# Time mixing beside small experts on one Trainium2 core: keys and decay computed once per chunk and spread through a DRAM scratch

## What is computed

```python
delta = shifted - x                      # shifted: the token before, zero at a sequence's start
low = jnp.tanh((x + delta * mu_x) @ W_x1).reshape(B, T, 5, PROJ_LR)
mus = jnp.einsum('blnr,dnr->blnd', low, W_x2) + x_bias
xr, xw, xk, xv, xg = [x + delta * mus[:, :, i] for i in range(5)]
r, k, v = xr @ W_r, xk @ W_k, xv @ W_v   # r, k: 16 heads x 4 keys; v: 16 heads x 8 values
w = -jnp.exp(jnp.tanh(xw @ W_w1) @ W_w2 + b_w2)
def step(S, inp):                        # S: 16 heads x 4 keys x 8 values
    r_t, k_t, v_t, w_t = inp
    o_t = jnp.einsum('bhk,bhkv->bhv', r_t, S) + jnp.einsum('bhk,hk,bhk,bhv->bhv', r_t, u, k_t, v_t)
    S = jnp.exp(w_t)[..., None] * S + k_t[..., :, None] * v_t[..., None, :]
    return (S, o_t)
# o: per head minus its mean, over its standard deviation; then
o = (o * gn_w + gn_b) * (g * jax.nn.sigmoid(g))      # g = xg @ W_g
return o @ W_o
```

## Time and profile before

| | us |
|---|---|
| runs shown | 4533.47, 4528.71, 4528.97 |
| median | 4528.97 |
| span of the profiled execution | 4561.0 |
| the last stage in it, from its first transfer issue (3721.9) | 839.1 |
| its 264 steps, first to last silu (3771.3 to 4545.2) | 773.9 |

### The profile page before, as it was taken

One profiled execution on the slowest core, in us unless ns is written; L12 is line 12 of the kernel. 1 busy time (PEld: TensorE's weight loads), 2 busy tenths in 40 slices (PEclk: granted clock), 3 DMA queues, 4 the chain that ended last, 5 costly groups with the idle time before them and its releaser, 6 DMA issues. The chain is left out here.

```text
span 4561.0 us, 88454 instructions
## 1 busy us (share of the span) xinstructions
PE 4030.3 (88%) x34698; PEld 2244.0 (49%) x34700; DVE 3477.9 (76%) x4781; ACT 2975.3 (65%) x4498; POOL 2360.6 (52%) x1443
## 2 busy tenths in 40 slices
PE   6999999999998989996877778887888868999998
PEld 3666666766676644451121211345777443444443
DVE  6888888888884557767889897466777747888888
ACT  3777777777775459953777777674565716555555
POOL 2878888888884013330221110461667526666665
PEclk7999999999999989986899999898999979999999
DMA  2212221221220011100210100331000323343433
GB/s 82 58 41 56 58 51 43 58 57 46 50 48 1 1 63 55 69 19 12 77 67 27 40 26 7 120 106 50 13 14 14 102 91 96 93 103 94 102 94 88
DMA packets 112123, 261.46 MB, mean 57 GB/s; under 512 B 24020, under 2 KB 35668, under 8 KB 110236
## 3 DMA queue, kind: packets, MB, share of 16 engines
q1 hardware_dynamic: 96292, 215.01, 17.3%
q0 software_dynamic: 15424, 40.89, 2.7%
HBM read 170.31 MB, written 49.76 MB: 48 GB/s over the span
## 5 line engine op out<-in xcount | busy, mean ns | idle before, releaser
L522 POOL TENSOR_TENSOR a_prob_low<-a_prob_whole,a_prob_high 128x1024 f16<-128x1024 f32 x512 | 1084.4, 2130 | 277.1 <-ACT a_prob_high L412 277.1
L496 DVE TENSOR_REDUCE a_part_max<-a_top 128x2 f32<-128x1024 f32 x512 | 626.2, 1223 | 218.3 <-PE a_top L323 212.4
L409 ACT ACTIVATE a_prob_whole<-a_score 128x1024 f32<-128x1024 f32 x512 | 524.9, 1025 | 332.5 <-PE a_score L312 320.4
L976 ACT ACTIVATE a_prob<-a_score 128x512 f32<-128x512 f32 x1024 | 533.1, 604 | 256.6 <-PE a_score L915 256.5
L1009 DVE TENSOR_REDUCE a_part_max<-a_side 128x2 f32<-128x1024 f32 x512 | 595.1, 1219 | 68.5 <-PE a_side L886 68.0
L2172 POOL TENSOR_TENSOR m_scaled<-m_acted,m_gate 128x512 f32<-128x512 f32 x264 | 433.2, 1649 | 269.4 <-DVE m_acted L2290 200.7
L412 ACT ACTIVATE a_prob_high<-a_score 128x1024 f16<-128x1024 f32 x512 | 522.3, 1020 | 0.0
L311 PE MATMUL a_score<-a_qa,a_ka 128*128 128x256 f16 x2048 | 476.1, 273 | 0.0
L312 PE MATMUL a_score<-a_qb,a_kb 128*128 128x256 f16 x2048 | 475.8, 273 | 0.0
L378 PE MATMUL a_o_ps<-a_v,a_prob_high 128*128 128x65 f16 x4096 | 428.7, 193 | 6.0 <-POOL a_prob_low L522 3.3
L380 PE MATMUL a_o_ps<-a_v,a_prob_high 128*128 128x64 f16 x4096 | 427.6, 194 | 0.0
(11 more groups left out here) (483 smaller groups left out, 10371.7 us busy)
## 6 DMA issues: line engine op xcount, KB each, us to landing
m_gate<-gates SPq DMA_DIRECT2D x264, 256.0 KB, 5.0
a_ka<-a_nat_high_k SPq DMA_DIRECT2D x128, 128.0 KB, 2.4
e_gate<-gates SPq DMA_DIRECT2D x8, 2048.0 KB, 7.1
slots<-in_slots SPq DMA_DIRECT2D x19, 520.0 KB, 4.3
a_qa<-a_nat_high_q SPq DMA_DIRECT2D x64, 128.0 KB, 2.4
a_qa<-a_nat_low_q SPq DMA_DIRECT2D x64, 128.0 KB, 2.4
a_qb<-a_nat_high_q SPq DMA_DIRECT2D x64, 128.0 KB, 2.4
a_kb<-a_nat_low_k SPq DMA_DIRECT2D x64, 128.0 KB, 2.4
```

The source lines that it names most:

```text
L409: eng.activation(prob_whole[:, e % RING, :, :, :], score[:, e % 2, :, :, :], ACT.Exp, scale=scale)
L496: eng.tensor_reduce(part_max[:, i, c, :, qt % 4], top[:, :, :], AX.X, ALU.max).then_inc(max_done, 1)
L522: eng.tensor_tensor(prob_low[:, e % RING, :, :, :], prob_whole[:, e % RING, :, :, :], prob_high[:, e % RING, :, :, :], ALU.subtract).then_ ...
L976: eng.activation(prob[:, e % RING, h, :], score[:, step % SLOTS, :], ACT.Exp).then_inc(exp_done, 1)
```

## The change

- r, k, w and v are made once per chunk: four matmuls (`w`, `k`, `r`, `v`) where there were 16; r, k and w fill 64 partitions (16 heads x 4 keys), v 128.
- ACT writes decay, k and r into `keys` [64 x 3 x 512] (`ew`, `decay`, `kc`, `rc`). SP stores it to a DRAM tensor `keys_d` (384 KB) and loads it back as `rep` [128 x 4 groups x 3 x 512] (3072 KB), each row of a head broadcast to its 8 value partitions. The loads of gate rows are now issued from a walk over the slots in which these two transfers have their places.
- `kv`j multiplies k in `rep` by `vs` in place, and `scan`j and `rs`j read decay and r from `rep`. `rs`j is the state times r alone.
- The term with u leaves the groups: `ruk` = r u k on 64 partitions (DVE), `bonus` sums it per head (PE), `av` = that times v (DVE), `oa` adds it into `o_ps`.
- `pick` becomes `center` (identity minus the mean over a head's 8 values), so `o_ps` is centred as it is accumulated: `o`, `mean` and `cen` go. `sq` reads `o_ps`; `eps` becomes the bias of `std`; the reciprocal is made in two halves; `norm` reads `o_ps`; `affine` moves to ACT. The group norm closes at slots 30 to 40 of the chunk, `LAST` goes, `PERIOD` is 33.

```diff
-    START, PERIOD = 12, 34
+    START, PERIOD = 12, 33
     PE_AT = {"low": 0, "low5": 1, "mu1": 2, "mu3": 3, "mu2": 4, "tanh_w": 5, "mu0": 6, "mu4": 7,
-             "w0": 8, "w1": 9, "v0": 10, "w2": 11, "w3": 12, "k0": 13, "r0": 14, "v1": 15, "k1": 16, "r1": 17, "o0": 18,
-             "v2": 19, "k2": 20, "r2": 21, "o1": 22, "v3": 23, "k3": 24, "r3": 25, "o2": 26, "g": 27, "o3": 28,
-             "mean": 30, "var": 33, "out": 63}
+             "w": 8, "k": 9, "r": 10, "v": 11, "g": 12, "bonus": 13, "o0": 23, "o1": 25, "o2": 27, "o3": 29, "oa": 30,
+             "var": 32, "out": 39}
-    ACT_AT = {"low": 1, "low5": 2, "wt": 6, "ew0": 10, "ew1": 10, "decay0": 10, "decay1": 10, "vs0": 11,
-              "ew2": 13, "ew3": 13, "decay2": 13, "decay3": 13, "vs1": 16, "vs2": 20, "vs3": 24,
-              "gs": 28, "o": 29, "sq": 32, "std": 36}
+    ACT_AT = {"low": 1, "low5": 2, "wt": 6, "ew": 9, "decay": 9, "kc": 10, "rc": 11, "vs": 12, "gs": 13,
+              "sq": 31, "std": 33, "affine": 37}
-    DVE_AT = {"z": -1, "mixed1": 3, "mixed3": 4, "mixed2": 5, "mixed0": 7, "mixed4": 8,
-              "kv0": 14, "carry0": 14, "scan0": 14, "u0": 15, "rs0": 15, "kv1": 17, "carry1": 17, "scan1": 17, "u1": 18, "rs1": 18,
-              "kv2": 21, "carry2": 21, "scan2": 21, "u2": 22, "rs2": 22, "kv3": 25, "carry3": 25, "scan3": 25, "u3": 26, "rs3": 26,
-              "cen": 31, "eps": 34, "rstd": 43, "norm": 45, "affine": 45, "gated": 47, "res": 64}
+    DVE_AT = {"z": -1, "mixed1": 3, "mixed3": 4, "mixed2": 5, "mixed0": 7, "mixed4": 8, "ruk": 12, "av": 14,
+              "carry": 19, "kv0": 20, "scan0": 21, "kv1": 22, "rs0": 22, "scan1": 23, "kv2": 24, "rs1": 24,
+              "scan2": 25, "kv3": 26, "rs2": 26, "scan3": 27, "rs3": 28,
+              "rstd0": 34, "rstd1": 35, "norm": 36, "gated": 38, "res": 40}
-    LAST = {"std": 35, "rstd": 36, "norm": 36, "affine": 36, "gated": 36, "out": 38, "res": 39}
+    KEEP_AT, SPREAD_AT = 12, 13
...
+                    c = (slot - KEEP_AT) // PERIOD
+                    if (slot - KEEP_AT) % PERIOD == 0 and c < CH:
+                        if c:
+                            eng.wait_ge(rep_in, 16 * c)
+                        after_act(eng, "rc", c)
+                        eng.dma_start(keys_d[:, :], keys[:, :, :]).then_inc(keys_out, 16)
+                    c = (slot - SPREAD_AT) // PERIOD
+                    if (slot - SPREAD_AT) % PERIOD == 0 and c < CH:
+                        after_dve(eng, "rs3", c - 1)
+                        eng.wait_ge(keys_out, 16 * (c + 1))
+                        eng.dma_start(rep[:, :, :], keys_d.rearrange("(h k) t -> h k t", k=GROUPS).unsqueeze(1).broadcast_to([16, 8, GROUPS, 3 * BANK])).then_inc(rep_in, 16)
...
-                        eng.matmul(o_ps[:, :], const["pick"][:, j, :], rs[:, j % 2, :], start=j == 0, stop=j == GROUPS - 1).then_inc(pe_done, 1)
+                        after_dve(eng, "av" if name == "oa" else f"rs{j}", c)
+                        eng.matmul(o_ps[:, :], const["center"][:, :], av[:, :] if name == "oa" else rs[:, j % 2, :],
+                                   start=name == "o0", stop=name == "oa").then_inc(pe_done, 1)
...
+                    elif name == "ruk":
+                        after_act(eng, "rc", c)
+                        after_pe(eng, "low5", c)
+                        op = eng.scalar_tensor_tensor(out=z[0:KEYS, :], in0=keys[:, W_R, :], scalar=cols[0:KEYS, U:U + 1],
+                                                      in1=keys[:, W_K, :], op0=ALU.mult, op1=ALU.mult)
...
-                        op = eng.tensor_tensor(kv[:, :], work[:, bank_of[f"k{j}", c], :], vs[:, j % 2, :], ALU.mult)
+                        if j == 0:
+                            after_act(eng, "vs", c)
+                            eng.wait_ge(rep_in, 16 * (c + 1))
+                        op = eng.tensor_tensor(rep[:, j, W_K * BANK:(W_K + 1) * BANK], rep[:, j, W_K * BANK:(W_K + 1) * BANK], vs[:, :], ALU.mult)
...
-                        op = eng.tensor_tensor_scan(st[:, j, 1:BANK + 1], decay[:, j, :], kv[:, :], st[:, j, 0:1], ALU.mult, ALU.add)
+                        op = eng.tensor_tensor_scan(st[:, j, 1:BANK + 1], rep[:, j, W_DECAY * BANK:(W_DECAY + 1) * BANK], rep[:, j, W_K * BANK:(W_K + 1) * BANK], st[:, j, 0:1], ALU.mult, ALU.add)
-                    elif name[0] == "u":
...
-                        op = eng.tensor_tensor(rs[:, j % 2, :], rs[:, j % 2, :], work[:, bank_of[f"r{j}", c], :], ALU.mult)
+                        op = eng.tensor_tensor(rs[:, j % 2, :], st[:, j, 0:BANK], rep[:, j, W_R * BANK:(W_R + 1) * BANK], ALU.mult)
...
+                        half = slice(j * BANK // 2, (j + 1) * BANK // 2)
+                        op = eng.reciprocal(std[:, half], std[:, half])
```

More of the change, by code:

```diff
@@ L1816, in mixing_and_experts @@
         gs = pl.sb("gs", [P, BANK])
-        vs = pl.sb("vs", [P, 2, BANK])
-        decay = pl.sb("decay", [P, GROUPS, BANK])
-        kv = pl.sb("kv", [P, BANK])
+        vs = pl.sb("vs", [P, BANK])
+        keys = pl.sb("keys", [KEYS, 3, BANK])
+        rep = pl.sb("rep", [P, GROUPS, 3 * BANK])
+        av = pl.sb("av", [P, BANK])
         st = pl.sb("st", [P, GROUPS, BANK + 1])
         rs = pl.sb("rs", [P, 2, BANK])
-        oz = pl.sb("oz", [P, BANK])
         cen = pl.sb("cen", [P, BANK])
-        sq = pl.sb("sq", [P, BANK])
         std = pl.sb("std", [P, BANK])
@@ L1880, in after_pool, with wait_bank @@
                 eng.wait_ge(pool_done, pool_no[name, c])
-        READER = {"low": (after_act, "low"), "low5": (after_act, "low5"), "tanh_w": (after_act, "wt"), "g": (after_act, "gs"),
-                  "mean": (after_dve, "cen"), "var": (after_dve, "eps"), "out": (after_dve, "res")}
-        READER.update({f"mu{i}": (after_dve, f"mixed{i}") for i in range(5)})
-        READER.update({f"{p}{j}": by for j in range(GROUPS) for p, by in
-                       (("w", (after_act, f"ew{j}")), ("v", (after_act, f"vs{j}")), ("k", (after_dve, f"kv{j}")), ("r", (after_dve, f"rs{j}")))})
+        def wait_bank(eng, name, c):
+            if (name, c) not in bank_user:
+                return
+            user, at = bank_user[name, c]
+            if user in IN_ACT:
+                after_act(eng, IN_ACT[user], at)
+            if user in IN_DVE:
+                after_dve(eng, IN_DVE[user], at)
+        IN_ACT = {"low": "low", "low5": "low5", "tanh_w": "wt", "w": "ew", "k": "kc", "r": "rc", "v": "vs", "g": "gs", "var": "std"}
+        IN_DVE = {"mu0": "mixed0", "mu1": "mixed1", "mu2": "mixed2", "mu3": "mixed3", "mu4": "mixed4", "bonus": "av", "out": "res"}
         def step_at(slot, lag):
@@ L1902, in store, with gate_rows @@
                     eng.dma_start(gates_d[:, pair * PAIR:(pair + 1) * PAIR], gates_t[:, pair % 2, :]).then_inc(stored[pair], 16)
-                for pair in range(2):
-                    store(pair)
-                for n in range(UNITS):
-                    for pair in range(CH // 2):
-                        g = n * (CH // 2) + pair
+                def gate_rows(g):
+                    n, pair = g // (CH // 2), g % (CH // 2)
+                    for j in range(J):
+                        for e in range(2):
+                            row = gates_d[2 * J * n + 2 * j + e:2 * J * n + 2 * j + e + 1, pair * PAIR:(pair + 1) * PAIR]
+                            eng.dma_start(gate[e * 64:e * 64 + 64, g % 2, j, :], row.broadcast_to([64, PAIR])).then_inc(gate_in[g % 2], 16)
+                store(0)
+                store(1)
+                eng.wait_ge(stored[0], 16)
+                gate_rows(0)
+                eng.wait_ge(stored[1], 16)
+                store(2)
+                store(3)
+                gate_rows(1)
+                for slot in range(SLOTS):
+                    g = (slot - START - UP_LAG) // (2 * J) + 1
+                    if (slot - START - UP_LAG) % (2 * J) == 0 and 2 <= g < UNITS * CH // 2:
+                        n, pair = g // (CH // 2), g % (CH // 2)
                         if n == 0:
                             eng.wait_ge(stored[pair], 16)
-                        if g == 1:
-                            store(2)
-                            store(3)
                         if pair == 2 and n + 1 < UNITS:
@@ L1916, in _ @@
                             eng.dma_start(w[:, :, :], w_d[n + 1, :, :, :]).then_inc(w_in, 16)
[L1917 to L1922 removed]
+                        eng.wait_ge(scaled_done, 2 * J * (g - 1))
+                        gate_rows(g)
+                    c = (slot - KEEP_AT) // PERIOD
[9 more added lines that the diff above has]
+                        eng.dma_start(rep[:, :, :], keys_d.rearrange("(h k) t -> h k t", k=GROUPS).unsqueeze(1).broadcast_to([16, 8, GROUPS, 3 * BANK])).then_inc(rep_in, 16)
                 for c in range(CH):
@@ L3023, in program @@
         sent2 = [pl.sem(f"sent2{r}") for r in range(2)]
+        keys_d = nc.dram_tensor("keys", (64, 3 * BANK), F32, kind="Internal").ap()
```

188 lines of the change are left out of this document (88 added, 100 removed).

## The result

The kernel after takes 4565.74 us (median of 4 runs, 4559.30 to 4573.47), the kernel before, beside it on the same chip, 4530.89 (4 runs, 4528.71 to 4533.47). The ratio is 1.0079, with a 95% interval of 1.0067 to 1.0091: slower by 0.8%, some 35 us, where 4510 was forecast. It lies above the range (4475 to 4548), on the side of rival (a).

A forecast was written before the change was run, and what follows sets the result against it. PE was taken to set the pace, with DVE a second bound right behind. Steps -13.5, end -7.3, start -1 and transfers +3 made -18.8: 4561.0 becomes 4542.2 profiled, 4510 from the median 4528.97; range 4475 to 4548.

The forecast's parts named there:

- rival (a): At kv0, `rep` arrives late from about 200 GB/s down; at 150 GB/s 70 us instead of 3, so 4577; chance 0.13.
- the steps: The last stage's 264 steps, first to last silu: 760.4 us against 773.9 before, a gain of 13.5.
- The end: After the last silu: 8.5 us with hand-overs instead of 15.8, a gain of 7.3.
- Slots 20 to 28: The stretch with kv, scans and rs: DVE sets the pace, 32.3 us per chunk, of which PE needs 20.0.
- the exclusion: A DVE operation with two SBUF operands and POOL's L2172 exclude each other; DVE pays about 1.20 us per slot waiting.
- Slots 29 to 13: Into the next chunk, 18 steps and 18 mixing matmuls: PE needs 50.4 us, DVE's 38.2 stays under it.
- the 3.5 of losses: Time lost per chunk beyond the engines' work: 3.5 us kept of 7.0, bounds 1.5 and 6.5.
- Slots 14 to 19: Six slots without mixing matmuls on PE: 6 x 1.94 = 11.6 us per chunk.
- The start: DVE's first z waits for the last constant; smaller constants gain 1 us, bounds 0 and 3.
- The transfers: Store of `keys`, load of `rep` at 405 GB/s: stalls of 0 to 2 us in chunks 2, 4, 6; +3 us.
- Rival (b), the clock: In slots 20 to 28 PE gets half the clock: +7.8 us per chunk, 4572; chance 0.07.
- Rival (c): No change: losses at their upper bound cost 24 us more; half of that gives 4520 to 4538; chance 0.22.

The follow-up runs named there:

- the kernel with both repairs: Changed kernel with `rep` loaded in four 768 KB loads, each with its own count, and the next unit's weights issued behind the earlier gate rows: 4521.70 us, ratio 0.9985.

## Why the prediction was wrong, step by step

Its own sum, made against the profile: the steps 760.4 with transfers left out, +3 for these, start -1, end -7.3.

- **The end** (-7.3): measured -7.2. Right.
- **Slots 20 to 28** (32.3): 31.5 in chunk 3 of after, where nothing is waited for, and 30.9 to 33.2, 31.9 on average, over the eight chunks of the kernel with both repairs. Right, and for the reason given: `kv` 1.75, scan 2.28, `rs` behind `kv` 0.68, DVE busy 31.50 of 31.50 in chunk 3. The run with v in PSUM agrees: without the reason the stretch is shorter by what its price says. Its -3 us per chunk was there to be found in the rows, and the prediction, which worked the exclusion out, didn't see that one operand left in PSUM avoids it.
- **Slots 29 to 13** (52.8 with the crossing and the 3.5 of losses): 51.8 to 53.3. Right.
- **Slots 14 to 19** (11.6): 12.5 to 13.5, 15.1 in chunk 3 even when its weights come in time. Too low: slot 14 takes 2.80 us from L2318 to L2318 and not 1.94, which is one mixing matmul (0.86) of slot 13 that lies on this side of the cut; the remaining 0 to 1 us per chunk, and 2.6 in chunk 3, isn't accounted for. The period without late transfers is then (4381.3 - 3891.3) / 5 = 98.0 us over chunks 2 to 6 of the kernel with both repairs, and not 96.7. Put to the term of the losses, which the sum had at 3.5 us a chunk, the 1.3 us make it 4.8, within its bounds of 1.5 and 6.5; that is 769.3 instead of 760.4 us of steps.
- **The start** (-1): +6.3. Missed outright. The prediction looked only at the wait for the constants; in the new order the first step stands behind chunk 0's k and r, which now come in slots 9 and 10, one bank after the other: DVE waited 9.1 us with `ruk` for `rc`, and `rc` 5.5 for PE (shown above). Every engine's first steps are in its queue behind this.
- **The transfers** (+3, bounds -3 to +25): 41.7 by the steps (811.0 - 769.3), 44.0 by the medians. This is the step that failed, in two places. The rate: the prediction chose the row of `e_gate`, 405 GB/s, because it too fills 128 partitions, over the 215 of the gate rows, and it wrote itself that the load "has a destination and a source like no other here". It priced the lower rate only at the stall of chunks 2, 4 and 6, from which came an upper bound of 25. At 206 GB/s `rep` takes 15.3 us and not 7.8. With a round of gate rows ahead of it in chunks 2, 4 and 6 DVE's waits there come to 25.4; for the other chunks the prediction had room, and they waited 11.1 in four. In chunk 1 `rep` is issued 5.5 us behind the store and not some 4 behind `rc`, and `kv0` starts 18 us after that. What PE and ACT lose before they are back in step comes on top of these 36.5. The queue: "in SP's queue the next gate rows stand behind `rep`", it says, and leaves out the load that also stands there in chunk 3, that of the weights: 26.0 us where the run that moves it has 15.1, and 12 to 13 us of the whole time by that run.
- **Rival (a)** named the place (`kv0`), the sign and the point from which it decides (about 200 GB/s). The measured 206 lies at that point, not at 150, and the time at 4566, not 4577. The chance of 0.13 was low for a cost whose nearest rows lay at 215 and 405, with the point of decision at 200 just below the lower one.
- **Rival (b), the clock:** the granted clock kept 1.00 through stretches with PE busy 21.9 of 31.5 and 23.0 of 32.8 us, and fell, to 0.92 and 0.77, only where PE sat through a wait; it was 0.97 in the stretch behind the longest. Right to give it little.
- **Rival (c)** is what the change is once its transfers are in time: 4521.7 to 4533 in the runs that repair or remove them, against 4529.

In the profiled executions the stage was to be 18.8 us shorter and was 36.2 longer. Of these 55.0 us 38.7 are the late transfers (41.7 less the 3 forecast), 8.9 the longer period, 7.3 the start and 0.1 the end. By the medians it is 55.7 us (4510 to 4565.7). The parts come from one profile of each kernel.

## What to carry to other kernels

- The rate of a load went with its shape here, not with its bytes or the width of its destination. A load into 128 partitions whose outer dimension is 16, each entry spread over 8 neighbours, ran at half the rate of one whose outer dimension is 128: 206 to 214 GB/s against 437. Where the nearest rows of a new transfer give two rates and the result turns on which of them holds, the range has to hold both results.
- An added load costs its neighbours in the queue as well: go through the queue slot by slot for all chunks and name what stands behind it, rare loads too. Here one load, seen late three times, cost 12 to 13 of the 42 us that late transfers took.
- Where a trace shows one product at two prices (here 1.75 us with both operands in SBUF beside GpSimd, 0.67 with one in PSUM), ask of each product which operand could stay in PSUM. Leaving v there was worth 20.8 us, where the change itself, its transfers in time, was worth 7. This change traded 9.5 us of PE's work a chunk for SBUF operands on DVE, and was worth only what DVE gave back.
